# Work moved ahead of two stage boundaries: retention's first tile and weights prepared in cross-attention, the first expert's weights in the feed-forward

## What is computed

```python
x = x + xattn(_layernorm(x), ctx)                 # 16 heads, threshold on the scores
a = _layernorm(x)                                 # "A" in the kernel
for i in range(2):                                # retention layers
    xn = layer_norm(a, ln1_scale[i], ln1_bias[i])
    y = group_norm(retention(xn, wq[i], wk[i], wv[i]), ...)
    tmp = xn @ Wg[i]
    a = tmp * sigmoid(tmp) * y @ Wo[i] + a
    a = gelu(layer_norm(a, ...) @ ffn_w1[i]) @ ffn_w2[i] + a
x = x + a
xf = _layernorm(x)
top_w, top_i = top_k(softmax(xf @ router_w.T), 2) # 2 of 8 experts for each token
out = x + sum of the two chosen experts' (silu(g) * u) @ w_down, weighted
```

## Time and profile before

| | us |
|---|---|
| median of 3 runs | 1757.0 (1753.85 to 1757.47) |
| the profiled execution | 1754.9 |
| its span | 1753.1 |
| TensorE busy | 1679.5 (96%) |
| VectorE, ScalarE, GpSimd busy | 1108.3, 855.0, 480.8 |
| TensorE's mean granted clock | 0.98 of full |

### The profile page before, as it was taken

One profiled execution on the slowest core, in us unless ns is written; L12 is line 12 of the kernel. 1 busy time (PEld: TensorE's weight loads), 2 busy tenths in 40 slices (PEclk: granted clock), 3 DMA queues, 4 the chain that ended last, 5 costly groups with the idle time before them and its releaser, 6 DMA issues.

```text
span 1753.1 us, 26244 instructions
## 1 busy us (share of the span) xinstructions
PE 1679.5 (96%) x9292; PEld 1443.5 (82%) x9292; DVE 1108.3 (63%) x2233; ACT 855.0 (49%) x1195; POOL 480.8 (27%) x356
## 2 busy tenths in 40 slices
PE   7999999999998599999998999999999999999997
PEld 6899999999998488878887887887887888888886
DVE  6555555455455567654336666635348999999995
ACT  4444444444343333335335233443335878787883
POOL 1443443443443244410002443300011313221211
PEclk9999999999999699999999999999988999999999
DMA  5101101101100410023225000222332533636622
GB/s 191 37 25 37 36 24 36 36 24 36 36 24 0 146 49 1 1 73 96 96 72 169 19 1 2 95 93 88 109 154 75 160 119 106 223 119 215 247 52 66
DMA packets 35253, 139.74 MB, mean 80 GB/s; under 512 B 4784, under 2 KB 5296, under 8 KB 28464
## 3 DMA queue, kind: packets, MB, share of 16 engines
q1 hardware_dynamic: 30016, 126.78, 20.3%
q0 software_dynamic: 5168, 12.06, 3.6%
HBM read 222.71 MB, written 12.85 MB: 134 GB/s over the span
## 4 chain that ended last, share of the span: by engine, by line
PE 57%; DVE 5%; DMA 2%; ACT 1%; issue 1%; SPq 0%; POOL 0%; DVEq 0%; POOLq 0%; ACTq 0%
PE bank L86 35%; PE bank L1451 9%; PE bank L1914 7%; PE bank L1346 2%; PE bank L1920 2%; DMA acc_d<-e_raw 1%; PE bank L1435 1%; DVE e_w L1835 1%; DVE rc L1100 1%; PE bank L1470 1%; DVE rs L1100 1%; DMA out<-acc_d 0%; PE bank L1358 0%; DVE r_xh L1067 0%; DMA wraw<-in_wa 0%
## 5 line engine op out<-in xcount | busy, mean ns | idle before, releaser
L1835 DVE TENSOR_TENSOR e_w<-e_raw,e_w 128x2048 fp32r<-128x2048 f32 x138 | 311.5, 2286 | 11.5 <-ACT e_w L1717 11.4
L1717 ACT ACTIVATE e_w<-e_raw 128x2048 fp32r<-128x2048 f32 x138 | 264.4, 1917 | 44.2 <-PE bank L1914 20.9
L86 PE MATMUL bank<-e_w,e_xT 128*128 128x512 f32 x1104 | 270.1, 394 | 0.5 <-DVE e_xT L1853 0.5
L86 PEld LDWEIGHTS bank<-e_w,e_xT 128*128 128x128 f32 x1104 | 203.9, 188 | 40.9 <-DVE e_xT L1853 0.7
L86 PE MATMUL bank<-x2T,fw 128*128 128x512 f32 x768 | 190.4, 398 | 4.7 <-DVE fw L1161 4.7
L86 PE MATMUL bank<-ctx,wk 128*128 128x258 f32 x1536 | 192.1, 284 | 0.0
L86 PE MATMUL bank<-wv,ctx 128*128 128x512 f32 x768 | 189.4, 395 | 2.4 <-DVE kT L575 2.4
L1451 PE MATMUL bank<-fw,hh 128*128 128x512 f32 x768 | 186.1, 392 | 3.0 <-DVE hh L1277 3.0
L86 PEld LDWEIGHTS bank<-ctx,wk 128*128 128x128 f32 x1536 | 186.6, 189 | 0.1
L86 PEld LDWEIGHTS bank<-x2T,fw 128*128 128x128 f32 x768 | 145.5, 191 | 36.0 <-issue 5.0
L1451 PEld LDWEIGHTS bank<-fw,hh 128*128 128x128 f32 x768 | 143.9, 188 | 34.9 <-issue 2.2
(11 more groups left out here) (232 smaller groups left out, 2767.6 us busy)
## 6 DMA issues: line engine op xcount, KB each, us to landing
e_raw<-in_we SPq DMA_DIRECT2D x138, 1024.0 KB
fraw<-in_wf SPq DMA_DIRECT2D x64, 512.0 KB, 3.5
ctxraw<-in_ctx SPq DMA_DIRECT2D x32, 514.0 KB, 3.6
wraw<-in_wa SPq DMA_DIRECT2D x20, 512.0 KB, 4.8
X<-in_x SPq DMA_DIRECT2D x4, 512.0 KB, 7.0
acc_d<-X SPq DMA_DIRECT2D x8, 256.0 KB, 3.1
xh_d<-A SPq DMA_DIRECT2D x8, 256.0 KB, 2.5
out<-acc_d SPq DMA_DIRECT2D x4, 512.0 KB, 5.9
```

The lines of the kernel that those rows point to most:

```text
L86: last = nc.tensor.matmul(out, lhs(t, a), rhs(t, b), start=start and n == 0, stop=n == len(steps) - 1)
L1717: nc.scalar.activation(w[pos][:, 0, :, :], raw[pos][:, :, :], ACT.Copy).then_inc(m["w_hi"], 1)
L1835: nc.vector.tensor_tensor(w[pos][:, 1, :, :], raw[pos][:, :, :], r(w[pos][:, 0, :, :]), ALU.subtract).then_inc(m["w_lo"], 1)
```

## The change

In cross-attention, the last token tile's batches also load retention's first eight half matrices (`ahead_load`), and behind the last key product four tables. In the last batch VectorE and GpSimd normalise the tiles that are finished. Tile 0 gets its second norm, is turned and split, q, k and v are split, and TensorE runs the products of tile 0 with q and k around its last product with `wo`. Buffers are placed by hand so that this does not overwrite what is in use (class `Ahead`). The bias of cross-attention is added to X before its product comes instead of after. Retention increments the semaphores of what is done already, and stores the zeros at its beginning.

In the second half of the last feed-forward, four pieces of expert 0 (G0, U0, G1, U1) are loaded one after the other into one buffer, and split in chunks 3, 6, 9 and 12. In the mixture only D0 and D1 remain to load; the four staged pieces are loaded again for tile 1, whatever its expert. VectorE waits until the first gather is issued before it splits D0. There are 7, 3, 3 and 3 spins between the turns of the router's tail, 6 instead of 10 behind it, and 14 instead of 24 before the first expert tile.

```diff
+STAGE_AT = (3, 6, 9, 12)
...
+                    sp.wait_ge(w_hi, DC + 3)
+                    sp.wait_ge(w_lo, DC + 3)
+                    for k in range(BPT):
+                        sp.wait_ge(ctx_hi, BPT * (NT - 1) + k - 1)
+                        sp.wait_ge(ctx_lo, BPT * (NT - 1) + k - 1)
+                        load(NT - 1, k)
+                        ahead_load(k)
+                    sp.wait_ge(v_ps, 2 * NB)
+                    sp.dma_start(ahead.lnv[:, :, :, :], a["lnv"][bass.ds(0, 1), :, :].rearrange("o p n -> p (o n)")).then_inc(tables_in, 16)
+                    sp.dma_start(ahead.rot[:, :, :], a["rot"]).then_inc(tables_in, 16)
+                    sp.dma_start(ahead.decay[:, :, :, :], a["decay"]).then_inc(tables_in, 16)
+                    sp.dma_start(ahead.gn_bc[:, :, :], a["gn"][bass.ds(0, 1), :, :, :].rearrange("o p k d -> p (o k) d")).then_inc(tables_in, 16)
+                    for j in range(WS, 2 * WS):
+                        sp.wait_ge(e["w_hi"], j - WS + 1)
+                        sp.wait_ge(e["w_lo"], j - WS + 1)
+                        ahead_load(j)
+                    for i in range(WS):
+                        sp.wait_ge(ahead_in[i], 32)
+                    sp.wait_ge(tables_in, 64)
...
-                            if k == 2 and not first:
-                                add_bias(it - 1)
+                            if k == 2:
+                                add_bias(it)
+                            if last and k == BPT - 1:
+                                ahead_root(slice(0, NT - 1), 1)
+                                ahead_root(slice(NT - 1, NT), 2)
                             normalise(b)
                     def add_bias(t):
-                        pool.wait_ge(x1_sum, t + 1)
+                        pool.wait_ge(xh_ok, NT)
                         xt = X[:, bass.ds(t, 1), :].rearrange("p o d -> p (o d)")
                         nc.gpsimd.tensor_tensor(xt, xt, bo_bc[:, :], ALU.add).then_inc(x1_ok, 1)
+                    def ahead_root(cols, n):
+                        pool.wait_ge(e["ve"], n)
+                        nc.gpsimd.tensor_tensor(a_rstd[:, cols], a_veps[:, cols], mhalf[:, 0:cols.stop - cols.start], ALU.pow).then_inc(e["rs"], 1)
...
+                    def ahead_hi(j):
+                        act.wait_ge(ahead_in[j % WS], 16 * (j // WS) + 16)
+                        act.wait_ge(qbd_ok, NB)
+                        w, half = ahead_w[j]
+                        nc.scalar.activation(w[:, 0, :, half * 256:(half + 1) * 256], ahead.wraw[j % WS][:, :, :], ACT.Copy).then_inc(e["w_hi"], 1)
...
+                    ahead_hi(0)
+                    ahead_hi(1)
                     turned(NB - 1)
+                    act.wait_ge(e["turned"], 1)
+                    act.wait_ge(w_lo, DC + 3)
+                    act.wait_ge(misc_in, 64)
+                    for c in range(DC):
+                        nc.scalar.activation(xf[:, c, :], bank[2][:, c * P:(c + 1) * P], ACT.Identity, scale=lnv[:, 0, 0, c:c + 1],
+                                             bias=lnv[:, 0, 1, c:c + 1]).then_inc(e["xf"], 1)
+                    act.wait_ge(e["xf"], DC)
+                    nc.scalar.activation(xn0[:, 0, :, :], xf, ACT.Copy).then_inc(e["xn_hi"], 1)
+                    ahead_hi(2)
+                    ahead_hi(3)
                     heads_hi(NT - 1)
+                    act.wait_ge(v_ps, 2 * NB)
+                    ahead_hi(4)
+                    ahead_hi(5)
...
+                            if final:
+                                dve.wait_ge(x1_measured, NT - 1)
+                                for t in range(NT - 1):
+                                    nc.vector.bn_aggr(a_mv[:, t, :], x1_stats[:, t, :]).then_inc(e["ag"], 1)
+                                dve.wait_ge(e["ag"], NT - 1)
+                                nc.vector.tensor_scalar(a_veps[:, 0:NT - 1], a_mv[:, 0:NT - 1, 1], 1e-5, None, ALU.add).then_inc(e["ve"], 1)
+                                dve.wait_ge(e["rs"], 1)
+                                ahead_rows(0)
                             threshold(b, (0, 1))
+                            if final:
+                                dve.wait_ge(e["a0"], 1)
+                                nc.vector.bn_stats(stats[:, 0, :], A[:, 0, :]).then_inc(e["st"], 1)
                             if not begin:
                                 last_token(b - 1)
+                            if final:
+                                dve.wait_ge(e["st"], 1)
+                                nc.vector.bn_aggr(a_mv[:, NT - 1, :], stats[:, 0, :]).then_inc(e["ag"], 1)
                             threshold(b, (2, 3))
+                            if final:
+                                dve.wait_ge(e["ag"], NT)
+                                nc.vector.tensor_scalar(a_veps[:, NT - 1:NT], a_mv[:, NT - 1, 1:2], 1e-6, None, ALU.add).then_inc(e["ve"], 1)
...
+                    dve.wait_ge(e["rs"], 2)
+                    nc.vector.tensor_scalar(xh[:, 0, :], A[:, 0, :], a_mv[:, NT - 1, 0:1], a_rstd[:, NT - 1:NT], ALU.subtract, ALU.mult).then_inc(e["xh"], 1)
+                    ahead_lo(0)
+                    ahead_lo(1)
                     last_token(NB - 1)
+                    ahead_rows(1)
+                    dve.wait_ge(e["xn_hi"], 1)
+                    nc.vector.tensor_tensor(xn0[:, 1, :, :], xf, r(xn0[:, 0, :, :]), ALU.subtract).then_inc(e["xn_lo"], 1)
                     heads(BPT - 1, NB - 1)
                     bias_heads(NT - 1)
+                    ahead_rows(2)
                     project_lo(NT - 1)
+                    for j in range(2, 6):
+                        ahead_lo(j)
+                    for t in range(3, NT - 1):
+                        ahead_rows(t)
                     add_x(NT - 1)
...
+                    pe.wait_ge(e["xh"], 1)
+                    pe.wait_ge(u_ok, DC * NB)
+                    for c in range(DC):
+                        last = nc.tensor.transpose(bank[2][:, c * P:(c + 1) * P], xh[:, 0, c * P:(c + 1) * P], ident[:, :])
+                    last.then_inc(e["turned"], 1)
                     pe.wait_ge(oT_ok, HPC * (NB - 1))
                     attend(BPT - 1, NB - 1, None)
+                    pe.wait_ge(e["xn_lo"], 1)
+                    pe.wait_ge(e["w_lo"], 2)
+                    products(nc, bank[0][:, :], range(DC), lambda c, h: xn0[:, h, c, :], lambda c, h: ahead.wq[:, h, c, :]).then_inc(e["q_ps"], 1)
                     project(NT - 1)
-def retention_layers(nc, a, whole, holder, sem, bank, X, A, ident, vec, mhalf, x1_stats, route, experts):
+                    pe.wait_ge(e["w_lo"], 4)
+                    products(nc, bank[1][:, :], range(DC), lambda c, h: xn0[:, h, c, :], lambda c, h: ahead.wk[:, h, c, :]).then_inc(e["k_ps"], 1)
...
+                sp.wait_ge(m["none_ok"], 1)
+                for spare in (route.xh_d, route.acc_d):
+                    sp.dma_start(spare[TOK:, :], xf[1][:, :, :].rearrange("p c n -> p (c n)")).then_inc(out_done[2], 16)
...
+                    if layer == L - 1:
+                        for c in range(FC):
+                            chunk_load(1, c, c % FS)
+                            if c % 3 == 0 and c >= 6:
+                                if c == 6:
+                                    sp.wait_ge(m["up_ps"], 2 * FC * layer + FC)
+                                experts.stage_load(sp, c // 3 - 2)
...
+                        if layer == L - 1 and c - FC in STAGE_AT:
+                            experts.stage_hi(act, STAGE_AT.index(c - FC))
...
+                            if first is not None and first + k in STAGE_AT:
+                                experts.stage_lo(dve, STAGE_AT.index(first + k))
...
+                    spin(nc, bank[R_BANK[t]], ident, 7 if t == NT // 2 else 3)
...
+            def stage_load(sp, i):
+                if i:
+                    sp.wait_ge(m["w_hi"], i)
+                    sp.wait_ge(m["w_lo"], i)
+                sp.dma_start(raw[G0][:, :, :], a["we"][0, PIECE_AT[staged[i]], :, :].rearrange("p (c n) -> p c n", c=DC)).then_inc(stage_in, 16)
+            def stage_hi(act, i):
+                act.wait_ge(stage_in, 16 * i + 16)
+                nc.scalar.activation(w[staged[i]][:, 0, :, :], raw[G0][:, :, :], ACT.Copy).then_inc(m["w_hi"], 1)
+            def stage_lo(dve, i):
+                dve.wait_ge(m["w_hi"], i + 1)
+                nc.vector.tensor_tensor(w[staged[i]][:, 1, :, :], raw[G0][:, :, :], r(w[staged[i]][:, 0, :, :]), ALU.subtract).then_inc(m["w_lo"], 1)
...
-                for pos in (G0, U0, G1, U1, D0):
+                for pos in (D0, D1):
                     sp.dma_start(raw[pos][:, :, :], a["we"][0, PIECE_AT[pos], :, :].rearrange("p (c n) -> p c n", c=DC)).then_inc(w_in[pos], 16)
-                sp.wait_ge(q["none_ok"], 1)
-                sp.dma_start(xh_d[TOK:, :], none).then_inc(q["none_stored"], 16)
-                sp.dma_start(acc_d[TOK:, :], none).then_inc(q["none_stored"], 16)
```

(31 more changed lines are left out.)

235 lines of the change are left out of this document (146 added, 89 removed).

## The result

The changed kernel takes 1742.21 us (median of 4 runs, 1739.22 to 1744.19) against 1755.84 us before: a ratio of 0.9917, 95% interval 0.99 to 0.9934. It is faster, but by about 14 us where 24 were forecast, and the time lies 3 us above the range. Six more runs later gave 0.9921 (0.9906 to 0.9936). The profiled execution has a span of 1742.4 us, 10.7 less than the one before (1753.1).

| event | before | after | difference |
|---|---|---|---|
| GpSimd's first normalise of cross-attention | 63.53 | 69.15 | +5.6 |
| its last one | 567.48 | 574.48 | +7.0 |
| end of g of the first retention tile | 617.06 | 608.34 | -8.7 |
| logits copied | 1302.23 | 1290.71 | -11.5 |
| matmuls of the counts | 1306.40 | 1293.11 | -13.3 |

A forecast was written before the change was run, and what follows sets the result against it. TensorE bounds the steady stretches; the change works at two boundaries where it idles at a lowered clock. Savings of 13.9 and 10.4 us, 24.3 off 1754.9, give 1730.6, taken as 1731; range 1726 to 1739.

The forecast's parts named there:

- B3: Second boundary, first gather: VectorE waits until it is issued, so it takes about 0.95 instead of 2.77 us, 1.8 less.
- A1 to A5: First boundary, cross-attention's end to retention's first g: five steps of the new order, ending g at 603.2, 13.9 us saved.
- rival four: End of cross-attention: held by the last weight load at 7.7 us, 2.1 us more, time 1733; chance 0.10.
- The feed-forward: Last feed-forward: four staged pieces add work on ScalarE and VectorE, one in each third chunk, all hidden: zero cost.
- B1: Router, second boundary: sixteen spins hold the clock at 2.4 GHz, so the counts start 4.4 us earlier.
- The rival of the falling clock: Router: the clock still falls, counts 1.2 us later than before, second boundary gives 4.8, time 1736; chance 0.15.
- B2: Second boundary: the gather follows the token table by 0.9 us without waiting for the zero rows, 6.6 us earlier in all.
- The rival "the first gather is slow": Second boundary: tile 1's four pieces, 4 MB, loaded just ahead of the gather, cost 3.5 us, time 1734; chance 0.10.
- B as a whole: Second boundary, last feed-forward chunk to the end of expert tile 0: 8.4 + 2.0 = 10.4 us saved, bounds 4 and 12.
- B5: Expert tile 0: gate and up pieces are ready, so it takes 23.1 instead of 25.1 us, 2.0 saved.
- A: First boundary, cross-attention's end to retention's first g: 13.9 us saved, bounds 11.8 and 16.3.
- the rival of the skill's page: First gather: takes 2.77 us for a reason of its own, not the split's; second boundary gives 8.6, time 1732.5; chance 0.03.

The follow-up runs named there:

- experiment 8: Changed kernel with four rows of the norm computed twice behind `wo`'s split: last normalise to the end of g 35.89 us instead of 33.86.
- experiment 1: Changed kernel with the increment behind the gather hung on a GpSimd memset: first gather takes 1.18 us, turn 7.99 us after the gather's start instead of 9.49.
- The kernel with both causes repaired: Changed kernel with both first-gather edits (memset increment, tile 1 loads wait for landing), hT at 22080, context tiles moved 128 bytes: 1732.79 us, ratio 0.987.

## Why the prediction was wrong

Three steps failed. B3 took for granted that VectorE waits until the gather is issued; it started ahead of it. Nothing stood in the sum for the 4 MB that now move beside the gather. And nothing stood in it for the untouched loops, whose matmuls became slower. By the prediction's own steps:

- **A1 to A5, the first boundary: right, a little too careful.** 15.7 us instead of 13.9, within the bounds of 11.8 and 16.3. With the 7.0 us by which all of it came later, the sum had `wo` ready at 587.45 (585.95 measured), statistics done at 595.6 (593.71), VectorE's first operation behind the barrier at 597.9 (596.22), the turn at 601.0 (599.09), g done at 610.2 (608.34). The 1.5 us at `wo` run through: the last product with v began 0.8 us earlier than the sum had it, and took 2.85 us where I kept today's 3.75, since the clock was half for less of this stretch (0.80 on average, 0.71 over the earlier trace rows's first). That the last load would be late (rival four) did not happen, by 0.9 us: experiment 8 shows VectorE in charge.
- **The feed-forward: right.** The half with the staged pieces took 86.95 us, 86.99 before. They cost nothing.
- **B1, the held clock: right.** 4.4 forecast, 4.4 measured (18.16 us from the last feed-forward matmul to the counts before, 13.73 after), 4.35 given back when the spins were taken away. The rival of the falling clock did not come true; where the clock did fall, in three of thirteen executions, it cost 0.2 to 0.3 us and not 4.
- **B2, no wait for the zero rows: right.** The gather starts 7.2 us earlier, 6.6 forecast; the rest is the table's sixteen matmuls, 2.13 us where they took 2.97, part of them at half clock.
- **B3, the undisturbed gather: wrong, the first step that failed.** I wrote "Now VectorE waits until it is issued, so it takes about 0.95". The price was right (1.18 in experiment 1) but VectorE does not wait. The increment is a queue instruction; it went out while GpSimd had not begun, and the split started 0.14 us ahead of the gather. Instead of 1.8 us won, 0.4 were lost. The Trainium skill, Perfetto Trace Analysis, section "Sequencer Loop", says that a sequencer pushes an engine's instruction into a queue and goes on to execute control instructions itself; the trace agrees, and I had read the diff, not asked which part of GpSimd does the increment.
- **The rival "the first gather is slow" was the truth, and I gave it 0.10.** Its price was good: 3.5 us, 3.8 measured. I had set, 12.2 us for a 1 MB load behind others, against "another queue". A queue of its own did not keep the gather clear of the loads: the core's 16 DMA engines were busy all the time (1.01 of the stretch, 423 GB/s) until it had landed. That it waits for its turn on these engines fits the windows, but is not shown. B as a whole brought 4.0 us instead of 10.4, the lower bound of the sum.
- **B5, tile 0: 1.4 us instead of 2.0.**
- **Nothing in the sum for the steady stretches: wrong.** I wrote that there "only fewer or faster matmuls would help, and the change removes none", and did not ask whether it could make them slower. The change moves nearly every buffer. That cost 2.7 us in the expert tiles and 1.4 in cross-attention, 0.7% and 0.3% of them.

In the profiled runs the difference between 24.3 and 10.7 is then: 5.6 of chance at the start, 6.4 in B, 4.1 of places, less 1.8 in A, less 0.7 in small pieces. The median lies 11.2 us above the forecast. Without the start these terms make 8.0 of them. The other 3.2 are not pinned to a cause: the mean first normalise of the thirteen executions, 66.4, is 2.9 us behind the 63.5 of the one execution on which the sum rests, but that one was the luckiest of all sixteen, and the stretch from g to the last feed-forward product varies as much. The kernel with both causes repaired measured 1732.8, where the forecast for what the change set out to do was 1731; that the two agree so well is in part luck, since A brought 1.8 us more than its sum.

On the rival of the skill's page: I had weighed the Trainium skill, SBUF — State Buffer, section "Who interferes with whom", which infers that a `tensor_tensor` with both inputs in SBUF leaves descriptor generation alone. Experiment 1 settles this for the gathers here: 3.20 beside the split and 1.18 without it for the first, 0.95 without and 3.02 beside it for the second. The measurement decides against the inference. Which of the two starts first decides: in the sixteen profiled executions all 130 gathers issued 0.09 us or more after such a split had begun ended 0.8 to 1.1 us behind its end, about what a gather takes alone, and the 206 during which a split began took 0.94 to 1.01 us.

## What to carry to other kernels

A signal that something has been *issued* must hang on work of the same engine behind it, not on an increment by its queue. When transfers are brought forward, list what they will now run beside: the one the critical path waits for should go first. And when a change moves buffers, compare the matmul cadence of the untouched loops before and after; here 0.7% of one loop of 392 us ate two thirds of the 4.0 us that the second boundary had brought.

## What the runs showed of the hardware

- **Operand places set the matmul's cadence.** At full clock and back to back, fp32 matmuls of 128 x 128 by 128 x 512 in the expert tiles start every 226.7 ns where the byte addresses of the two SBUF operands leave the same remainder of 256, and every 233 to 234 ns where they leave different ones (128 or 192 against 64). All rows of the table fit, the seven slow matmuls behind a slow product granted (within these tiles every piece begins at a multiple of 512 bytes), and moving hT from 16576 to 16704 switched the loss off. The mechanism behind it is not shown. Both kernels hold more such pairs, which bear the rule out. The products of `r_wo` (64) with `yT` (128) start a matmul every 233.3 ns on average (waits left out), those of `r_wk` and `r_wg` (64) with `xn` (64) every 226.9. A feed-forward layer's first half reads `x2T0` at 212864 (128), its second `x2T1` at 120384 (64), against weights at 64; a product takes 2.76 us in the first and 2.72 in the second. The down products of the first half have equal remainders themselves, but each stands behind a slow up product. The rows are of the kernel before:

```profile
782.04 2.93 PE L86 MATMUL bank<-x2T,fw 128*128 128x512 f32 x12
784.80 2.94 PE L1451 MATMUL bank<-fw,hh 128*128 128x512 f32 x12
...
1209.53 2.88 PE L86 MATMUL bank<-x2T,fw 128*128 128x512 f32 x12
1212.25 2.88 PE L1451 MATMUL bank<-fw,hh 128*128 128x512 f32 x12
```

By these rows, about 4 us more could be won in either kernel (an estimate: 64 products at 0.04 us and 16 of `r_wo` at 0.08); no run tried it. The Trainium skill, TensorE: Matmul & The Clock Gate, section "Step-by-step: what each phase is for", says that the two operands come through two independent read ports and that loading the next weights takes nothing from the running matmul; no run here takes the weight loads apart, but with different remainders the same matmuls and loads take 3% longer, which the section does not have. In cross-attention a shift of the context tiles by 128 bytes brought back 1.4 us; there the rows are 258 columns long, so the remainder changes within a tile, and everything behind the tiles moved as well. Whether it is the same effect was not tried.
- **A gather beside 4 MB of other loads landed 3.8 us later,** though SyncE's loads and GpSimd's gather are on different queues; the core's DMA engines were busy 1.01 of that stretch, 0.57 without the loads.
- **A gather issued during a VectorE subtraction of 128 x 2048 ends 0.8 to 1.1 us behind it,** whatever is left of the subtraction; one that began first takes 0.94 to 1.01 us, and one with no split beside it 0.94 to 1.18 (368 gathers in sixteen executions; two issued 0.01 us behind a split's start took 0.95 all the same).
- **When the clock first rises and falls is chance.** It rose at 11.5 to 12.7 us in some executions and at 23.3 to 25.0 in others, of one and the same kernel too; the same start took 65.0 to 69.2 us to the first normalise. Full clock from 4.5 us on did not help, because it fell again at 14.7 us during small matmuls. The Trainium skill, TensorE: Matmul & The Clock Gate, section "What's actually happening", says that the number of slow matmuls at a kernel's start varies from run to run; the profiled runs agree.
